# Fourth feed-forward stage of a four-layer kernel: sorted rows that carry x and s, and a finish four tiles at a time

## What is computed

```python
def _L3_ffn_ref(hidden_states, wg_red, wg, w1, b1, w2, b2):
    x = hidden_states.reshape(-1, c)
    xr = x @ wg_red.T
    wg_unit = wg / jnp.maximum(jnp.linalg.norm(wg, axis=1, keepdims=True), EPS)
    logits = xr @ wg_unit.T
    gates = jax.nn.softmax(logits, axis=1)
    indices_s = jnp.argmax(gates, axis=1)
    scores = jnp.max(gates, axis=1)
    for e in range(E):
        mask = (indices_s == e).astype(x.dtype)[:, None]
        h = jax.nn.gelu(x @ w1[e] + b1[e], approximate=False)
        out = out + mask * (h @ w2[e] + b2[e])
    out = out * scores[:, None]
...
xn = _layernorm(x, axis=-1)
s = _L3_attn_ref(xn, L3_attn_W)
g = _silu(_L3_ffn_ref(xn, ...))
x = x + s * g
```

## Time and profile before

| | us |
|---|---|
| median of three runs | 6293.48 |
| lowest and highest | 6290.90 and 6296.18 |
| the profiled execution, device time | 6286.02 |
| its span, from the first to the last event | 6284.30 |
| PE busy in the span | 5663.1 (90%) |
| DVE, ACT, POOL busy | 4362.2, 3824.9, 2909.5 |

### The profile page before, as it was taken

One profiled execution on the slowest core, in us unless ns is written; L12 is line 12 of the kernel. 1 busy time (PEld: TensorE's weight loads), 2 busy tenths in 40 slices (PEclk: granted clock), 3 DMA queues, 4 the chain that ended last, 5 costly groups with the idle time before them and its releaser, 6 DMA issues. The chain is left out here.

```text
span 6284.3 us, 101861 instructions
## 1 busy us (share of the span) xinstructions
PE 5663.1 (90%) x33881; PEld 3000.5 (48%) x33881; DVE 4362.2 (69%) x9909; ACT 3824.9 (61%) x8008; POOL 2909.5 (46%) x2782
## 2 busy tenths in 40 slices
PE   8999999599997999999999799999999999887653
PEld 3444444322222666666666444444444444465453
DVE  4555554277875777777878588888888888685624
ACT  2444444166665777777777577777777777564322
POOL 1225325467776766666766333323223323244355
PEclk9999999799998999999999899999999999999876
DMA  2001001311101111111111100000000000031324
GB/s 46 15 15 41 23 25 35 104 34 41 31 27 36 41 34 31 31 31 43 47 41 42 41 11 19 11 12 19 12 16 14 12 19 9 26 89 42 109 69 123
DMA packets 361193, 230.25 MB, mean 37 GB/s; under 512 B 28386, under 2 KB 338658, under 8 KB 360418
## 3 DMA queue, kind: packets, MB, share of 16 engines
q1 hardware_dynamic: 343072, 191.96, 11.8%
q0 software_dynamic: 10240, 21.25, 1.1%
q10 hardware_dynamic: 7362, 10.52, 0.5%
HBM read 104.43 MB, written 76.94 MB: 29 GB/s over the span
## 5 line engine op out<-in xcount | busy, mean ns | idle before, releaser
L3827 PE MATMUL a_scores_ps<-a_kT,a_q_mixed 128*128 128x512 f32 x2048 | 1046.4, 593 | 3.2 <-ACT a_probs L3637 3.1
L3837 PE MATMUL a_acc_ps<-a_probsT,a_v_post 128*128 128x512 f32 x2048 | 1042.8, 592 | 0.4 <-DVE a_probsT L3730 0.4
L3637 ACT ACTIVATE a_probs<-a_scores_ps,a_neg_max 128x512 f32<-128x512 f32 x1024 | 703.1, 687 | 428.6 <-DVE a_neg_max L3720 419.2
L3720 DVE TENSOR_REDUCE a_neg_max<-a_scores_ps 128x1 f32<-128x512 f32 x1024 | 693.4, 677 | 201.8 <-PE a_scores_ps L3827 197.1
L3730 DVE STREAM_TRANSPOSE a_probsT<-a_probs 128x512 f32<-128x512 f32 x1024 | 715.6, 699 | 135.8 <-PE a_acc_ps L3837 112.5
L3642 ACT ACTIVATE a_probs<-a_probs,a_inv_sum 128x512 f32<-128x512 f32 x1024 | 727.7, 711 | 0.8 <-DVE a_inv_sum L3725 0.8
L3008 DVE TENSOR_REDUCE a_neg_max<-a_pair_ps 128x2 f32<-128x1024 f32 (+3 forms) x512 | 417.8, 824 | 357.5 <-PE a_pair_ps L3104 352.5
L2813 ACT ACTIVATE a_probsT<-a_pair_ps 128x1024 f32<-128x1024 f32 (+3 forms) x512 | 359.4, 704 | 485.1 <-PE a_pair_ps L3117 483.6
L3837 PEld LDWEIGHTS a_acc_ps<-a_probsT,a_v_post 128*128 128x128 f32 x2048 | 389.0, 190 | 490.9 <-issue 488.8
L3827 PEld LDWEIGHTS a_scores_ps<-a_kT,a_q_mixed 128*128 128x128 f32 x2048 | 384.4, 190 | 476.0 <-issue 437.5
L3583 POOL TENSOR_TENSOR a_q_mixed<-a_qT,a_pre 128x512 f32<-128x512 f32 x248 | 250.3, 1042 | 759.0 <-PE a_scores_ps L3827 759.0
(11 more groups left out here) (418 smaller groups left out, 11826.6 us busy)
## 6 DMA issues: line engine op xcount, KB each, us to landing
f_v_even<-f_v_odd SPq DMA_DIRECT2D x224, 130.0 KB, 2.3
attention_out<-a_s_out SPq DMA_DIRECT2D x64, 256.0 KB, 2.3
a_v<-a_v_rows SPq DMA_DIRECT2D x256, 64.0 KB, 2.1
f_x<-x_after SPq DMA_DIRECT2D x48, 256.0 KB, 5.5
f_gx<-x_after SPq DMA_DIRECT2D x48, 256.0 KB, 3.5
f_gs<-attention_out SPq DMA_DIRECT2D x48, 256.0 KB, 3.6
routes_y_rows<-a_zeros SPq DMA_DIRECT2D x32, 256.0 KB, 2.8
a_parts<-routes_y_rows SPq DMA_DIRECT2D x32, 256.0 KB, 3.5
```

Source lines behind the costliest of these rows:

```text
L3637: act.activation(probs[:, n % NPR, :], scores_ps[n % NS][:], ACT.Exp, bias=neg_max[:, n % NS:n % NS + 1], scale=1.0, accum_out=row_sum[:, ...
L3720: dve.tensor_reduce(neg_max[:, n % NS:n % NS + 1], scores_ps[n % NS][:], AX.X, ALU.max, negate=True).then_inc(max_ready, 1)
L3827: pe.matmul(scores_ps[n % NS][:], q_mixed[:, g % 2, i].rearrange("f a q -> f (a q)"), kT[:, par, :], start=True, stop=True).then_inc(score ...
L3837: pe.matmul(acc_ps[par][:], v_post[:, g, i, :], probsT[:, g % NT, i, :], start=(p == 0), stop=(p == U - 1)).then_inc(products_done, 1)
```

## The change

The DRAM tensor of sorted rows now belongs to an object that both phases know. A row has 386 floats in place of 128: the normalised x, the token's own row number (HOME), half the softmax weight (HALF), x and s. The fill moves into the attention phase, two stores of 128 x 4 x 386 floats in each of nine steps; a filled row has a HOME beyond the output. SP loads x a second time and s (32 loads) into the wide rows in SBUF, and the 64 scatters wait for them. The weight is computed ahead of the slots.

In the tile loop `add_b1` is gone: ACT adds b1 as the bias operand of four GELUs of 128 columns each. When the four tiles of a group have their b2, DVE and ACT finish the group in four steps, one per tile period: times half the weight (`weigh`), times s (`scale_s`), tanh on ACT, (tanh + 1) times that (`gate_s`), plus x (`add_x`). This is y * sigmoid(y) written as half y times (1 + tanh of half y). POOL then scatters the 128 rows of each tile to the output by their HOME, eleven tiles behind its copy of w1, which has three buffers in place of four. Rows beyond the output are dropped (`bounds_check`). A group's load waits until the group four earlier is finished. The store to `y_sorted`, the gathers and the whole finish are gone.

```diff
+    WIDE, X, S, HOME, HALF = 3 * D + 2, slice(D + 2, 2 * D + 2), slice(2 * D + 2, 3 * D + 2), D, D + 1
...
 (attention phase, SP)
+                if n == 0:
+                    sp.wait_ge(fill_ready, 1)
+                if 0 <= n < 9:
+                    for g in range(2 * n, min(2 * n + 2, GROUPS)):
+                        sp.dma_start(sorted_rows.x_groups[g], fill[:]).then_inc(filled, 16)
...
 (expert phase, SP)
-            sp.wait_ge(zeros_ready, 1)
-            for g in range(GROUPS):
-                sp.dma_start(x_groups[g], zeros[:]).then_inc(zeroed, 16)
+            for b in range(batches):
+                sp.dma_start(x[:, b, :, X], x_rows[b]).then_inc(s_loaded, 16)
+                sp.dma_start(x[:, b, :, S], s_rows[b]).then_inc(s_loaded, 16)
...
                 if g >= 4:
-                    sp.wait_ge(tile_turned, (g - 3) * GROUP)
+                    sp.wait_ge(y_kept, g - 3)
+                    sp.wait_ge(homes_ready, g - 3)
                 sp.dma_start(x_tiles[:, g % 4], x_groups[g]).then_inc(tiles_loaded[g % 4], 16)
...
 (POOL)
-            pool.wait_ge(zeroed, 16 * GROUPS)
             pool.wait_ge(slots_ready, 1)
+            pool.wait_ge(s_loaded, 32 * batches)
...
-                if i >= 4:
-                    pool.wait_ge(hidden_done, i - 3)
-                pool.tensor_copy(w1_now[:, i % 4], w1[:, bass.ds(e, I)]).then_inc(w1_picked, 1)
...
-                    pool.indirect_dma_start(y[:, b % 4, c, :], None, y_sorted,
-                                            bass.IndirectOffsetOnAxis(ap=slot[:, n:n + 1], axis=0)
-                                            ).then_inc(gathered[b % 4], 16)
+                if i >= 3:
+                    pool.wait_ge(hidden_done, i - 2)
+                pool.tensor_copy(w1_now[:, i % 3], w1[:, bass.ds(e, I)]).then_inc(w1_picked, 1)
+
+            def scatter_tile(i):
+                g, t = divmod(i, GROUP)
+                if t == 0:
+                    pool.wait_ge(homes_ready, g + 1)
+                pool.wait_ge(y_kept, g + 1)
+                pool.indirect_dma_start(out_flat, bass.IndirectOffsetOnAxis(ap=homes[:, i:i + 1], axis=0),
+                                        y_tiles[:, g % 4, t, :], None, bounds_check=N * P - 1,
+                                        oob_is_err=False).then_inc(y_scattered[g % 4], 16)
+
+            for i in range(TILES + SCATTER_LAG):
+                if i < TILES:
+                    pick_w1(i)
+                if i >= SCATTER_LAG:
+                    scatter_tile(i - SCATTER_LAG)
...
 (ACT)
-                act.wait_ge(inner_ready, i + 1)
+                e = act.value_load(at_k[0:1, i:i + 1], min_val=0, max_val=(E - 1) * K)
+                act.wait_ge(hidden_done, i + 1)
...
-                act.activation(hidden[:, i % 4], inner[:, i % 2], ACT.Gelu).then_inc(hidden_ready, 1)
+                for k in range(K):
+                    last = act.activation(hidden[:, i % 4, k * P:(k + 1) * P], hidden_ps[i % 4][:, k * P:(k + 1) * P],
+                                          ACT.Gelu, bias=b1[:, bass.ds(e + k, 1)])
+                last.then_inc(hidden_ready, 1)
+
+            def tanh_of(g):
+                act.wait_ge(weighed, g + 1)
+                act.activation(gate[:, g % 2], y_group[:, g % 2], ACT.Tanh).then_inc(tanh_ready, 1)
...
 (DVE)
+            def weigh(g):
+                dve.wait_ge(y_biased, (g + 1) * GROUP)
+                dve.tensor_tensor(y_group[:, g % 2], y_group[:, g % 2],
+                                  x_tiles[:, g % 4, :, HALF:HALF + 1].to_broadcast([P, GROUP, D]),
+                                  ALU.mult).then_inc(weighed, 1)
...
+                chain(dve.tensor_tensor(scaled[:, g % 2], y_group[:, g % 2], x_tiles[:, g % 4, :, S], ALU.mult))
...
+                chain(dve.scalar_tensor_tensor(scaled[:, g % 2], gate[:, g % 2], 1.0, scaled[:, g % 2], ALU.add, ALU.mult))
...
+                dve.tensor_tensor(y_tiles[:, g % 4], scaled[:, g % 2], x_tiles[:, g % 4, :, X], ALU.add).then_inc(y_kept, 1)
...
+            for i in range(TILES + GROUP + 1):
+                if 0 <= i - 2 < TILES:
                     add_b2(i - 2)
+                if i < TILES and i % GROUP == 2:
+                    homes_of(i // GROUP)
+                if i > GROUP:
+                    g, step = divmod(i - GROUP - 1, GROUP)
+                    (weigh, scale_s, gate_s, add_x)[step](g)
```

More of the change, by code:

```diff
@@ L1465, in sorted_experts_phase @@
         weight = sb("weight", [P, N])
-        zeros = sb("zeros", [P, GROUP, D])
-        x_tiles = sb("x_tiles", [P, 4, GROUP, D])
+        x_tiles = sb("x_tiles", [P, 4, GROUP, WIDE])
         xT_tile = sb("xT_tile", [D, 2, P])
-        w1_now = sb("w1_now", [D, 4, I])
-        inner, hidden = sb("inner", [P, 2, I]), sb("hidden", [P, 4, I])
-        y_tiles = sb("y_tiles", [P, 2, GROUP, D])
-        gx, gs, y = sb("gx", [P, 2, NC, D]), sb("gs", [P, 2, NC, D]), sb("y", [P, 4, NC, D])
-        gate, out = sb("gate", [P, 2, NC, D]), sb("out", [P, 2, NC, D])
+        w1_now = sb("w1_now", [D, 3, I])
+        hidden = sb("hidden", [P, 4, I])
+        xT, redT = hidden[:, 0:2], hidden[0:GR, 2:4]
+        y_group, gate, scaled = (sb(name, [P, 2, GROUP, D]) for name in ("y_group", "gate", "scaled"))
+        logits, diff = (gate[:, n].rearrange("p g d -> p (g d)")[:, 0:E * N].rearrange("p (n e) -> p n e", e=E)
+                        for n in range(2))
+        first, running = (scaled[:, n].rearrange("p g d -> p (g d)")[:, 0:E * N].rearrange("p (e n) -> p e n", e=E)
+                          for n in range(2))
+        y_tiles = sb("y_tiles", [P, 4, GROUP, D])
         turn_ps = [ps("turn0"), ps("turn1")]
@@ L1645, in _ @@
             chain = Chain(dve, dve_chain)
-            dve.memset(zeros[:], 0.0).then_inc(zeros_ready, 1)
             dve.memset(ones[:], 1.0)
@@ L1652, in moments_of @@
                 for c in range(NC):
-                    last = dve.bn_stats(stats[:, b % 2, c, :], x[:, b, c, :])
+                    last = dve.bn_stats(stats[:, b % 2, c, :], x[:, b, c, 0:D])
                 chain(last)
@@ L1670, in _ @@
             dve.wait_ge(weights, 16 * (len(loads) + 1))
+            dve.tensor_copy(x[:, :, :, HOME], home[:].rearrange("p (b c) -> p b c", c=NC))
             chain(dve.tensor_tensor(wg_sq[:], wg[:], wg[:], ALU.mult))
@@ L1707, in _ @@
             dve.tensor_tensor(count[:, 1:E], ends[:, 1:E], ends[:, 0:E - 1], ALU.subtract).then_inc(counted, 1)
+            dve.wait_ge(exp_ready, 1)
+            chain(dve.tensor_reduce(weight[:], diff[:], AX.X, ALU.add))
+            chain(dve.reciprocal(weight[:], weight[:]))
+            dve.tensor_scalar(x[:, :, :, HALF], weight[:].rearrange("p (b c) -> p b c", c=NC), 0.5, None, ALU.mult)
             dve.wait_ge(summed, 1)
@@ L1750, in add_b2 @@
                 dve.wait_ge(y_done, i + 1)
-                if t == 0 and g >= 2:
-                    dve.wait_ge(y_stored[g % 2], 16 * (g // 2))
-                dve.tensor_tensor(y_tiles[:, g % 2, t, :], y_ps[i % 2][:, 0:D], b2[:, bass.ds(e, D)],
-                                  ALU.add).then_inc(y_kept, 1)
-            for i in range(TILES + 2):
-                if i < TILES:
-                    add_b1(i)
-                if i >= 2:
-                    add_b2(i - 2)
-            def scale(b):
-                dve.wait_ge(gathered[b % 4], 16 * NC * (b // 4 + 1))
-                w = weight[:, b * NC:(b + 1) * NC].unsqueeze(2).to_broadcast([P, NC, D])
-                dve.tensor_tensor(y[:, b % 4], y[:, b % 4], w, ALU.mult).then_inc(y_scaled, 1)
@@ L1777, in _ @@
-            for b in range(batches + 1):
-                if b < batches:
-                    scale(b)
-                if b >= 1:
-                    finish(b - 1)
+                dve.tensor_tensor(y_group[:, g % 2, t], y_ps[i % 2][:, 0:D], b2[:, bass.ds(e, D)],
+                                  ALU.add).then_inc(y_biased, 1)
+            def weigh(g):
[3 more added lines that the diff above has]
+                                  ALU.mult).then_inc(weighed, 1)
@@ L1842, in up @@
                 if i >= 4:
-                    pe.wait_ge(inner_ready, i - 3)
+                    pe.wait_ge(hidden_ready, i - 3)
                 for k in range(K):
-                    last = pe.matmul(hidden_ps[i % 4][:, k * P:(k + 1) * P], w1_now[:, i % 4, k * P:(k + 1) * P],
+                    last = pe.matmul(hidden_ps[i % 4][:, k * P:(k + 1) * P], w1_now[:, i % 3, k * P:(k + 1) * P],
                                      xT_tile[:, i % 2], start=True, stop=True)
@@ L1911, in upper_attention_phase @@
         s_out = sb("s_out", [P, 2, NC, D])
+        fill = sb("fill", [P, sorted_rows.GROUP, sorted_rows.WIDE])
         x_ps, v_ps = ps("x"), ps("v")
@@ L2080, in _ @@
             rows.before_loop(dve)
+            chain(dve.memset(fill[:], 0.0))
+            dve.memset(fill[:, :, sorted_rows.HOME], float(sorted_rows.NOWHERE)).then_inc(fill_ready, 1)
             dve.memset(ones[:], 1.0)
```

143 lines of the change are left out of this document (57 added, 86 removed).

## The result

The changed kernel takes 6231.62 us (median of 4 runs, 6227.38 to 6234.53) against 6294.83 (4 runs, 6290.90 to 6298.03): ratio 0.9899, 95% interval 0.9882 to 0.9916. The forecast was 6210.8 with a range of 6201 to 6240. The range held it, the likeliest case (6203 to 6218) did not; what came is close to the first rival, with a longer tail.

A forecast was written before the change was run, and what follows sets the result against it. The feed-forward stage was taken as routing, 80 us scatter, 137 us PE, 100 us gather and finish, PE working only in the third. 0.7 + 0.4 + 0.5 + 1.8 + 2 - 88.1 = -82.7 from 6293.48 gave 6210.8, range 6201 to 6240.

The forecast's parts named there:

- the likeliest case: Whole kernel: the forecast by itself, without any rival, 6203 to 6218 us, chance 0.62.
- the first rival: Tile loop: collisions with DVE operations do not settle, so POOL sets the period; 6220 to 6231 us, chance 0.22.
- Fills, 0: Attention stage: 18 fills of 790 KB, two per step, fit between SP's loads and cost 0.
- Routing, +1.1: Before the scatters: one more small load and a DVE copy, +0.7 us; softmax weight moved ahead of the slots, +0.4.
- Scatters, 0 for the width, +0.5 for landing: The 64 scatters of sorted rows: 1544 bytes a row instead of 512 cost POOL nothing; the last lands 0.5 us later.
- slope: Scatters of sorted rows: POOL's time grows with row width, +66 us, 6277, or half of it, 6244; chance 0.06.
- pieces: Scatters of sorted rows: each row is cut into four descriptors and POOL pays for each, +185 us, 6396; chance 0.02.
- First group, +1.8: First tiles: the awaited first group load grows from 256 KB to 790 KB, +1.8 us.
- Loop, +2: Tile loop: PE's period stays 1.90 us, with POOL's work at 1.80; +2 us in all for stumbles.
- the pattern: Tile loop: DVE's group operation ends about when POOL's copy starts, and the scatter starts before the next, so nothing collides.
- Tail, 12.4: After the last matmul: 8.3 us to POOL's last scatter issue, 0.5 for collisions, 3.6 to the end; 12.4 replaces 100.5, -88.1.

The follow-up runs named there:

- the GELU in one piece: The changed kernel with one GELU of 512 columns per tile instead of four of 128, first-layer bias left out: loop 149.7 us against 152.8, stage 325.8 us.
- the kernel with twelve: The changed kernel with POOL scattering a tile twelve copies behind instead of eleven: 6204.75 us against 6279.30 before the change, ratio 0.9877.

## Why the prediction was right, and where not

- **Fills, 0:** right, 230.5 against 231.0, and again with twice as many.
- **Routing, +1.1:** +0.7. The weight stands where the forecast put it, 5963.54 to 5965.07 in after, and the scatters waited for DVE's slots (25.3 us) and not for the 32 loads.
- **Scatters, 0 for the width, +0.5 for landing:** 967 ns each against 963, first scatter to first load +0.6. The rivals on the width, slope and pieces, fall.
- **First group, +1.8:** +1.6.
- **Loop, +2:** +12.9. This step failed. Of the difference 2.2 us are at the start (gaps of 2.76, 1.92, 4.63 against 2.67, 1.92, 2.49), where the first table load stood ahead of the GELU's wait and now stands behind it: the forecast counted the second load as saved and did not ask where the first one now stands. That the GELU is nearer to PE is not the reason, since the GELU in one piece is as near and keeps its load ahead. 7.9 us are the last 51 periods, 2.051 against 1.896, and 2.7 the last tiles behind them, of which 1.5 are the pause of PE that four of the six traces with this pattern of periods do not have. The forecast had every duration of the loop without collisions right (POOL 1.80, ACT's 1.14 + 0.30 under its 1.86) and the pattern too, as the kernel with twelve shows. What it left out is how POOL gets into the pattern: the first scatter is due behind the twelfth copy and POOL waits 2.07 us for the first group there. That this wait decides is shown by the twelve; how it does so is read from the timelines: with 0.1 us to spare per tile POOL cannot catch up without passing through the place where copy and group operation meet, and there it is thrown back.
- **The first rival,** POOL sets the loop, had 0.22 and is what happened, by its mechanism. Its price per tile was 2.05 at the low end, and 2.051 was measured. That is partly luck: it gave the copy and the scatter 0.125 each, where the scatter has 0.01 and the copy 0.24.
- **Tail, 12.4:** 18.7, a term mis-sized in two halves. POOL's last scatter began 10.8 us after the last matmul, where the sum has it begin at 8.8: the first scatter of the last group but one waited 2.98 us for its group. That wait belongs to PE's pause; in the four traces without the pause there is no such wait, the last scatter begins 10.2 after the last matmul and the tail is 18.1. And 7.9 us follow its beginning, 7.0 its end, where I took 3.6 from the earlier trace rows, an end with a store behind a DVE operation. The DRAIN behind POOL's scatter was not in the sum, though the trace of before has it, exposed, at 1230.03.
- **The rule on the shared ports.** The Trainium skill, SBUF — State Buffer, section Who interferes with whom, has the later instruction wait for the whole of the earlier. The rule has the pair right (DVE with two SBUF inputs, a POOL instruction that reads SBUF). Who pays depends on the offset, as these rows of after show:

```profile
6083.47 0.68 DVE L1760 TENSOR_TENSOR f_scaled<-f_y_group,f_x_tiles 128x512 f32<-128x512 f32 x1
6083.57 1.04 POOL L1569 COPY f_w_now<-f_w 128x512 f32 x1
...
6090.90 0.68 DVE L1760 TENSOR_TENSOR f_scaled<-f_y_group,f_x_tiles 128x512 f32<-128x512 f32 x1
6091.11 1.32 POOL L1576 DMA_INDIRECT out<-f_y_tiles,f_homes  x1 [0.17 <-issue]
...
6092.44 0.62 POOL L1569 COPY f_w_now<-f_w 128x512 f32 x1
6092.55 1.06 DVE L1764 SCALAR_TENSOR_TENSOR f_scaled<-f_gate,f_scaled 128x512 f32<-128x512 f32 x1
```

When copy and group operation start 0.1 us apart (first and third pair) only the later one grows, by 0.4, which agrees with the rule in direction, though the earlier had 0.5 to 0.6 to go. When the copy starts 0.3 to 0.7 us into the group operation, as in most of the loop, both grow: the copy takes 0.96 to 0.98 and the operation ends 0.51 after the copy's start. The same section infers that the preparing of descriptors needs the write side, which such an operation leaves free. The scatters agree with that when they start ahead of the operation (at most 1.00 us in 673 of 674 cases, over the twelve kernels with full group operations). They do not when they start inside it (second pair, and the gather of the earlier trace rows): started 0.03 to 0.5 us into it they take 1.51 down to 1.05, so that they end about 1.54 us after its start.

- **The whole:** -82.7 forecast, -66.0 by the marks, -63.2 by the medians.

## What to carry to other kernels

A pattern that fits into a period on paper holds only if the queue enters it in step: where an engine has a few per cent to spare, look at its first wait after the start, and give it one more stage of distance. One number, eleven to twelve, was worth 10 us here, as much as all collisions together. What an instruction brings with it (a table load, a register read) can stand ahead of its wait, where it is hidden, or behind it, where it costs; after a change, look on which side it stands. And what closes a phase depends on the engine that works last: look for a place in the old trace that ends the way the new kernel will.

## What the hardware showed that I had not expected

- A POOL copy of 128x512 that starts 0.3 to 0.7 us into a DVE operation with two SBUF inputs of that size takes 0.97 in place of 0.62 us, and the operation 0.79 to 1.21 in place of 0.69. When they start 0.1 us apart the later one alone grows, to 1.04 (copy) or 1.06 (DVE).
- An indirect scatter leaves that DVE operation at 0.68 us. It grows itself, to as much as 1.51, when it starts inside the operation, and not when it starts ahead of it.
- An indirect scatter of 1544 bytes a row costs POOL 967 ns, one of 512 bytes 963.
- POOL's DRAIN at the end of a phase ends 5.3 us (at two places in before) to 6.0 us (in after) after the end of an indirect DMA that is POOL's last work, in bounds or not, though the rows landed 1.1 us after it.
- Unchanged code moved by 11 us between two executions, in one phase of the second layer, in which engines show waits that end by no event of the trace.
